# Two attention layers, a state-space block and six transformer layers in one kernel: convolution spread over more steps, other homes for its buffers, second layer's weights loaded in step 6

## The reference

```python
x = x + L0_attn(xn) + L0_ffn(xn)            # first layer, xn = layernorm(x)
xn = layernorm(x)
x = x + L1_attn(xn) + L1_ffn(xn)            # second layer

def L1_attn(x):                             # state-space block, ED = 256, K = 15, N = 16
    h = layernorm(x) * gamma + beta
    xin, z = split(h @ W_in.T + b_in)
    xc = silu(causal_conv(xin, conv_w, 15 taps, per channel) + conv_b)
    dt, B, C = split(xc @ W_x.T)
    delta = softplus(dt @ W_dt.T + b_dt)
    # scan over 2048 rows: h = h * exp(delta * A) + delta * B * xc ; y = sum(h * C)
    return x + ((y + xc * D_param) * silu(z)) @ W_out.T + b_out

def L1_ffn(x):                              # six layers
    for i in range(6):
        x = local_attention(shift_tokens(x), 16 heads of 64, window 32) + x
        x = gelu_gated_ffn(layernorm(shift_tokens(x)), inner 341) + x
    return x
```

## Time and profile before

| | us |
|---|---|
| time, median of 3 runs | 3064.14 (3058.77 to 3069.75) |
| the profiled execution's own time | 3057.84 |
| its span | 3056.0 |
| TensorE busy | 2839.6 (93%) |
| VectorE busy | 2302.5 (75%) |
| ScalarE busy | 1753.7 (57%) |
| GpSimd busy | 1673.7 (55%) |

### The profile page before, as it was taken

How to read it: one execution, slowest core, us unless ns; L and a number is a source line. 1 busy time by engine, 2 the same in 40 slices (tenths; PEclk the granted TensorE clock), 3 DMA queues, 4 the chain that set the end, 5 groups by cost and what they waited for, 6 DMA issues and landing times.

```text
span 3056.0 us, 98277 instructions
## 1 busy us (share of the span) xinstructions
PE 2839.6 (93%) x41012; PEld 1864.1 (61%) x41012; DVE 2302.5 (75%) x3659; ACT 1753.7 (57%) x2614; POOL 1673.7 (55%) x1459
## 2 busy tenths in 40 slices
PE   6999999989999998899799999999999999999996
PEld 5556556555665655566466666666666666666664
DVE  2777666584677776799577888889888888788873
ACT  2545555545666665455466666666666666666663
POOL 0000001100466665565476888788887888788862
PEclk7999999999999999999899999999999999999998
DMA  2000000000011211132324334333433343333331
GB/s 92 1 1 1 1 1 1 3 1 10 19 46 47 45 46 49 47 100 73 95 72 117 92 85 111 85 97 79 111 88 92 89 109 92 82 94 82 81 76 50
DMA packets 181801, 188.21 MB, mean 62 GB/s; under 512 B 77614, under 2 KB 128564, under 8 KB 179956
## 3 DMA queue, kind: packets, MB, share of 16 engines
q1 hardware_dynamic: 181364, 181.94, 23.5%
HBM read 60.99 MB, written 6.03 MB: 22 GB/s over the span
## 4 chain that ended last, share of the span: by engine, by line
PE 48%; issue 5%; DVE 3%; POOL 2%; ACT 1%; DMA 1%; SPq 0%; ACTq 0%; DVEq 0%; POOLq 0%
PE ps L1366 15%; PE ps L1374 5%; PE ps L1417 5%; PE ps L1459 5%; PE ps L1381 4%; PE ps L1426 2%; PE ps L1473 2%; PE ps L1480 2%; PE ps L1407 2%; PE ps L1474 2%; PE ps L1390 1%; POOL ra L2002 1%; PE ps L1443 1%; DVE ss L1854 1%; DVE acc L483 1%
## 5 line engine op out<-in xcount | busy, mean ns | idle before, releaser
L1366 PE MATMUL ps<-wqkv,xcT 128*128 128x512 f32 x1152 | 559.7, 609 | 52.5 <-issue 31.9
L594 PE MATMUL ps<-xnT,qp 128*128 128x512 f32 (+3 forms) x1280 | 529.4, 544 | 16.2 <-ACT prob L819 15.3
L1983 POOL TENSOR_TENSOR ra<-ra,rb 128x1024 f32<-128x1024 f32 x192 | 452.0, 2360 | 134.3 <-DVE rb L1847 133.6
L819 ACT ACTIVATE prob<-ps,ebias,shift 128x1024 f32<-128x1024 f32 (+7 forms) x384 | 360.4, 954 | 142.7 <-DVE ebias L710 74.3
L827 ACT ACTIVATE probT<-ps 128x512 f32<-128x512 f32 (+3 forms) x384 | 207.6, 541 | 354.4 <-PE ps L607 354.2
L594 PEld LDWEIGHTS ps<-xnT,qp 128*128 128x128 f32 x1280 | 233.0, 192 | 274.5 <-issue 228.5
L2002 POOL TENSOR_TENSOR ra<-ra,rn 128x1024 f32<-128x1024 f32 x192 | 361.3, 1902 | 7.8
L1366 PEld LDWEIGHTS ps<-wqkv,xcT 128*128 128x128 f32 x1152 | 196.2, 190 | 220.8 <-issue 209.3
L701 DVE TENSOR_REDUCE nmx<-ps 128x1 f32<-128x1024 f32 (+7 forms) x256 | 245.7, 986 | 111.1 <-PE ps L594 96.7
L1626 ACT ACTIVATE sq<-ps 128x1024 f32<-128x1024 f32 x192 | 195.1, 1016 | 93.7 <-PE ps L1366 93.4
L1845 DVE TENSOR_TENSOR ra<-ps,tab 128x1024 f32<-128x1024 f32 x192 | 233.1, 1214 | 5.9 <-issue 5.5
(11 more groups left out here) (274 smaller groups left out, 5739.0 us busy)
## 6 DMA issues: line engine op xcount, KB each, us to landing
vw<-vs SPq DMA_DIRECT2D x576, 130.0 KB
vw<-vs SPq DMA_DIRECT2D x384, 65.0 KB
bc<-bc_scratch SPq DMA_DIRECT2D x128, 128.0 KB, 3.1
area<-bc_scratch SPq DMA_DIRECT2D x128, 128.0 KB, 4.3
wqkv<-lwqkv_dram SPq DMA_DIRECT2D x6, 1536.0 KB, 8.8
xc<-xs SPq DMA_DIRECT2D x96, 32.0 KB
wo<-lwo_dram SPq DMA_DIRECT2D x6, 512.0 KB, 9.8
area<-ys SPq DMA_DIRECT2D x24, 128.0 KB
```

The costliest lines, as they stand in the source:

```text
L594: mm = E.matmul(ps[:, 2 * r + o // 512, 0:w], k.qp[:, group % 2, g % NTH * P:(g % NTH + 1) * P], k.xnT[:, k0 + o:k0 + o + w], start=True, ...
L819: A.activation(k.prob[:, r, 0:nk], ps[:, 2 * r:2 * r + 2, :].rearrange("p a b -> p (a b)")[:, 0:nk], ACT.Exp, bias=k.ebias[:, row % 2:row ...
L1366: mm = E.matmul(to[:, c, :], k.xcT[:, n % 4, :], k.wqkv[l % 2][:, at + 512 * c:at + 512 * (c + 1)], start=True, stop=True)
L1983: G.tensor_tensor(k.ra[:, n % 2, w, :], k.ra[:, n % 2, w, :], k.rb[:, w, :], ALU.add).then_inc(s("added_" + what), 1)
```

## The change

```diff
-CONV = [(0, t) for t in range(3)] + [(a, t + 3 * (1 - a)) for t in range(KC - 3) for a in (1, 0)] + ...
-CONV_FIRST, CONV_LAST = 3, 11
-IN_STEPS = {2: 0, 3: 1, 4: 2, 5: 3}
-SILU_STEP, FACTOR_STEP, RATE_STEPS = CONV_LAST + 1, CONV_LAST + 2, {CONV_LAST + 4: 0, CONV_LAST + 5: 1}
+TAPS = {3: 3, 4: 3, 5: 3, 6: 2, 7: 3, 8: 3, 9: 2, 10: 2, 11: 3, 12: 3, 13: 2, 14: 1}
+IN_EXTRA, IN_LATE = {3: 1, 4: 3}, {2: 0, 3: 2}
+HAT_STEP, SILU_STEPS, FACTOR_STEP, RATE_STEPS = 2, {9: 0, 15: 1}, 15, {16: 0, 17: 1}
...
-FIRST_UNIT = 21
+FIRST_UNIT = 22
@@ transformer_sp
-            S.wait_ge(s("conv"), ET)
+            S.wait_ge(s("saved"), 16)
         load_projections(k, l)
...
-    def save_gate(m):
-        S.wait_ge(s("in_out"), 2 * ET + 2 * m + 2)
-        S.dma_start(k.mz_d[:, m, :], k.mz1 if m else k.mz0).then_inc(s("saved"), 16)
+    def save_gates():
+        S.wait_ge(s("in_out"), 4 * ET)
+        S.dma_start(k.mz_d, k.mz).then_inc(s("saved"), 16)
...
-        if n % NT == (CONV_LAST + 1 if n < NT else 2) and n // NT + 1 < L:
+        if n % NT == (6 if n < NT else 2) and n // NT + 1 < L:
             load_layer(n // NT + 1)
...
         if n == 4:
-            save_sum()
-            save_gate(0)
-        if n == 5:
-            S.wait_ge(s("saved"), 16)
             load_forward(0)
-            save_gate(1)
-        if n == SILU_STEP:
+        if n == 5:
+            save_sum()
+            save_gates()
+        if n == max(SILU_STEPS):
             save_convolved()
-        if n == FACTOR_STEP:
+        if n == FACTOR_STEP + 1:
             save_factors()
-        if n == max(RATE_STEPS):
+        if n == max(RATE_STEPS) + 1:
             save_rates()
@@ transformer_pe
-        if n == 1:
+        if n == HAT_STEP:
             turn_hat()
-        if n in IN_STEPS:
-            E.wait_ge(s("small"), 80)
-            project_in(n, IN_STEPS[n])
+        if n in IN_EXTRA:
+            project_in("extra", n, IN_EXTRA[n])
         if n < NTILE:
             values(n, 1)
         if n + 1 < NTILE:
             turn_rows("q", n + 1)
             turn_rows("k", n + 1)
+        if n in IN_LATE:
+            E.wait_ge(s("small"), 80)
+            project_in("late", n, IN_LATE[n])
@@ transformer_act (the evictions follow their projections)
-        if n == SILU_STEP:
-            convolved()
+        if n in SILU_STEPS:
+            convolved(SILU_STEPS[n])
@@ transformer_dve, before the steps
         if n == 0:
+            V.wait_ge(s("rotated_k"), 1)
+            V.tensor_tensor(k.ra[:, 0, 1, :], k.ra[:, 0, 1, :], k.rb[:, 1, :], ALU.add).then_inc(s("added_k"), 1)
             residual_dve(k, pair("out", 0))
@@ in the steps
-        if n == 1:
-            normal_dve(k)
         if n + 2 < NTILE:
             rotate("q", n + 2)
...
-        for i in taps[2:]:
-            conv_dve(k, i)
+        for a, t in taps[2:]:
+            conv_dve(k, a, t)
+        if n == 1:
+            normal_dve(k)
@@ transformer_pool
+    G.wait_ge(s("fixed"), 32)
+    G.tensor_copy(k.band[:], k.band32).then_inc(s("band"), 1)
     for n in range(2):
         add("q", n)
         better(n)
         normal("q", n)
-        add("k", n)
+        if n:
+            add("k", n)
         normal("k", n)
-        if n == 0:
-            G.wait_ge(s("fixed"), 32)
-            G.tensor_copy(k.band[:], k.band32).then_inc(s("band"), 1)
-            G.tensor_copy(k.mxp[:, :, 0:PAD], k.tail[:]).then_inc(s("padded"), 1)
...
-        if n in (2, 3):
+        if n in (3, 4):
@@ build
-            k.mxp = here.take(P, ET, PAD + TH)
+            k.mz = here.take(P, ET, TH)
...
+            beside = here.take(P, PAD + TH)
+            k.dec = sb("dec", [P, PAD + TH], c=c)[:]
+            k.mxp = (beside, k.dec)
```

More of the change, by code:

```diff
@@ L1033 @@
 TURNED = NT // 4
-CONV = [(0, t) for t in range(3)] + [(a, t + 3 * (1 - a)) for t in range(KC - 3) for a in (1, 0)] + [(1, t) for t in range(KC - 3, KC)]
-CONV_FIRST, CONV_LAST = 3, 11
-IN_STEPS = {2: 0, 3: 1, 4: 2, 5: 3}
-SILU_STEP, FACTOR_STEP, RATE_STEPS = CONV_LAST + 1, CONV_LAST + 2, {CONV_LAST + 4: 0, CONV_LAST + 5: 1}
+TAPS = {3: 3, 4: 3, 5: 3, 6: 2, 7: 3, 8: 3, 9: 2, 10: 2, 11: 3, 12: 3, 13: 2, 14: 1}
+IN_EXTRA, IN_LATE = {3: 1, 4: 3}, {2: 0, 3: 2}
+HAT_STEP, SILU_STEPS, FACTOR_STEP, RATE_STEPS = 2, {9: 0, 15: 1}, 15, {16: 0, 17: 1}
+assert sum(TAPS.values()) == ET * KC
 def conv_share(n):
[L1042 to L1047, removed]
+    done = sum(TAPS[i] for i in TAPS if i < n)
+    return [divmod(i, KC) for i in range(done, done + TAPS.get(n, 0))]
 def heads_dve(k):
@@ L1701, in turned_hat, with projected_in, convolved @@
         A.wait_ge(s("turned"), TURNED + 3 + q)
[L1702 to L1716, removed]
+        A.activation(k.mxT[:, q * 512:(q + 1) * 512], pair("extra", HAT_STEP)[:, q, :], ACT.Identity, bias=k.cols[:, 1:2], scale=k.cols[:, 0:1]).then_inc(s("turned_out"), 1)
+    def projected_in(place, n, m):
+        for q in range(2):
+            of = pair(place, n)[:, q, :]
+            A.wait_ge(s("in_mm"), 2 * m + q + 1)
+            if m < ET:
+                A.activation(k.mxp[m][:, PAD + q * 512:PAD + (q + 1) * 512], of, ACT.Identity, bias=k.cols[:, 2 + m:3 + m]).then_inc(s("in_out"), 1)
+            else:
+                A.activation(k.mz[:, m - ET, q * 512:(q + 1) * 512], of, ACT.Silu, bias=k.cols[:, 2 + m:3 + m]).then_inc(s("in_out"), 1)
+    def convolved(a):
+        A.wait_ge(s("conv"), a + 1)
+        A.activation(k.mu[:, a, :], k.mu[:, a, :], ACT.Silu).then_inc(s("mu"), 1)
     def factors(n):
-        A.wait_ge(s("saved"), 32)
         for q in range(2):
@@ L1724, in rates @@
     def rates(n, a):
-        A.wait_ge(s("saved"), 48)
+        A.wait_ge(s("saved"), 32)
         A.wait_ge(s("dt_mm"), a + 1)
@@ L1778, in transformer_act @@
             gelu(m, int(what[2]))
[L1779 removed]
+        if n == HAT_STEP:
             turned_hat(0)
             turned_hat(1)
[L1782 to L1786 removed]
+        if n in IN_EXTRA:
+            projected_in("extra", n, IN_EXTRA[n])
+        if n in SILU_STEPS:
+            convolved(SILU_STEPS[n])
         if n + 1 < NTILE:
@@ L1791, in transformer_act @@
             out_turned(n)
+        if n in IN_LATE:
+            projected_in("late", n, IN_LATE[n])
         if n == FACTOR_STEP:
@@ L1795, in transformer_act @@
             rates(n, RATE_STEPS[n])
-        if what and what != "turn_normal" and n < NTILE or IN_STEPS.get(n, 0) >= ET:
+        if what and what != "turn_normal" and n < NTILE or IN_EXTRA.get(n, 0) >= ET or IN_LATE.get(n, 0) >= ET:
             A.preload_act_table_set("natural_log_exp_and_others")
@@ L1915, in transformer_dve @@
         taps = conv_share(n)
-        for i in taps[:2]:
-            conv_dve(k, i)
+        for a, t in taps[:2]:
+            conv_dve(k, a, t)
         if n < NTILE:
@@ L2031, in rest_sum @@
         here = k.acc[:, NTH:NT, :]
-        if step == 2:
+        if step == 3:
             G.wait_ge(s("ln_done"), 2)
@@ L2088, in transformer_pool @@
             deviations()
-        if n in (2, 3):
-            if n == 3:
+            for a in range(ET):
+                ins = G.tensor_copy(k.mxp[a][:, 0:PAD], k.tail[:, a, :])
+            ins.then_inc(s("padded"), 1)
+        if n in (3, 4):
+            if n == 4:
                 G.wait_ge(s("g"), rest)
```

40 lines of the change are left out of this document (18 added, 22 removed).

## The result

The changed kernel takes 3020.6 us (median of four runs, 3019.0 to 3029.3) where the kernel before takes 3065.3 beside it (four runs, 3058.8 to 3069.8): the ratio is 0.9862, with a 95% interval of 0.9835 to 0.9888. The profiled execution took 3019.65 us around a span of 3017.8, so the two profiles differ by 38.2 us, against 36.1 predicted. The medians of this comparison differ by 44.7, but its ratio and those of two later comparisons of the same kernels (e4, e9) are 0.9862, 0.9877 and 0.9880, which is 37 to 42 us of 3064.

The account below looks back on a forecast made before the run. The prediction took TensorE, busy 93% of the span, as the bound, with VectorE binding steps 3 to 9 and a stall in step 11. Its terms summed to -36.1 us, giving 3028 us from a median of 3064.14; range 3010 to 3047.

Parts of the forecast that it names:

- The stall: Steps 10 to 12: loading the second layer in step 6 ends GpSimd's wait for its scales and TensorE's behind it; -23.9 us.
- near 18: Sign that the prediction is right: step 11 takes near 18 us at a clock of 1.00.
- The load's price: Step 6: the second layer's load makes TensorE stand on "issue" in its value matmuls; +1.5 us, bounds 0 and 7.8.
- Norm's scaling: Steps 1 and 2: scaling behind step 1's softmax work, transposes in step 2, end the waits for GpSimd's powers; -6.4 us.
- Taps: Steps 3 to 9: convolution taps spread over steps 3 to 14 shorten steps where VectorE is late; -5.7 us, bounds 0 and -12.5.
- steps 4 to 6 each below 18.2: Sign that the prediction is right: steps 4, 5 and 6 each take less than 18.2 us.
- Steps 13 to 18: These steps gain three taps and one half's SiLU; +1.5 us (0.5 SiLU, 1.0 step 13's two taps), bounds -4 and +7.
- Band's cast: Start of the second part: the mask's cast ahead of GpSimd's first addition ends TensorE's 3.14 us stand; -3.1 us.
- the later scan: All 64 scan units one step later, with the same instructions; 0 us, bounds -5 and +5.
- (a): Rival, steps 3 to 14: long TensorE steps pay back VectorE's lateness, 10 us more, -46, 3018 us; chance 0.13.
- (b): Rival: trailing taps wait for GpSimd's additions in seven steps (3, 4, 5, 7, 8, 11, 12), 2.0 us each; 3042 us; chance 0.13.
- (c): Rival: only the stall of step 11 and its clock go, -20, VectorE stays as late; 3044 us; chance 0.08.

Follow-up runs that it names:

- e4: The changed kernel itself, run again beside the kernel before: 3024.0 us, ratio 0.9877.
- e9: The changed kernel itself, run once more beside the kernel before: 3023.1 us, ratio 0.9880.
- e3: The changed kernel with the second layer's whole load moved back from step 6 to step 12: 3036.3 us, ratio 0.9918 to the kernel before.
- e1: The kernel before with only the second layer's scales' transfer moved to step 6, weights still in step 12: 3041.6 us, ratio 0.9933.
- e6: The changed kernel with the norm's scaling back ahead of step 1's rotations, its transposes staying in step 2: 3027.8 us, ratio 0.9895 to the kernel before.
- e11: The changed kernel with the second layer's whole load in one go in step 8 instead of 6: 3020.3 us, ratio 0.9864 to the kernel before.
- e10: The changed kernel with the second layer's scales in step 6, its weights in four pieces in steps 7 to 10: 3018.8 us, ratio 0.9860.
- e12: The changed kernel with its load in pieces and one tap moved from step 5 to step 14: 3015.4 us, ratio 0.9847 to the kernel before.
- e5: The changed kernel with the old distribution of taps (4, 4, 4, then six times 3, steps 3 to 11): 3027.3 us, ratio 0.9890.
- e2: The kernel before with only the scan's first unit moved from step 21 to step 22: 3059.3 us, ratio 0.9992.
- e7: The changed kernel with the mask's cast behind the first keys' normalising and their addition on GpSimd again: 3025.0 us, ratio 0.9883 to the kernel before.

## Why the prediction was right, and where it was off

**The stall (-23.9; measured -23.5): right, mechanism and size.** Put back alone it costs 20.8 us in step 11 (e3), taken away alone it gives 20.5 there (e1). Step 11 is 18.85 us at a clock of 1.00, with "near 18" expected, and steps 10 and 12 are 19.4 and 18.4 for 19.7 and 18.3.

**The load's price (+1.5; measured 3.2 to 4.3): the mis-sized term.** It was taken from one stand of 1.5 us beside the third layer's load in step 18. The same step of the kernel before has a second one, and as much moving as step 6 has now:

```profile
1600.55:1623.40 22.85, 18.86 (x355) 13.92 (x356) 13.36 (x20) 8.70 (x13) 17.19 (x19) 1.00 0.72 206
...
PE ps L1417 <- issue: 1.5, 1, 1.5
PE ps L1381 <- issue: 1.4, 1, 1.4
```

So the row was half of what that load cost there, and 22.85 us is 2.8 more than the 20.0 that step 18 takes after. The prediction also left out the clock: the stand of 2.75 us in step 6 put the transposes behind it at half the clock, 1.2 us more.

**Norm's scaling (-6.4; measured -6.7): right in sum.** Step 1 is 17.5 for 16.4 and step 2 17.8 for 19.2: step 2 absorbed more of the transposes than was booked, and step 1 paid VectorE's 17.26 us of work, which is 1.5 more than the 15.72 it was priced by. One instruction explains it. The scaling's first half, 1.23 us where nothing ran beside it, now stands beside GpSimd's two additions and takes 3.03:

```profile
1255.12 4.70 POOL L1980 TENSOR_TENSOR ra<-ra,rb 128x1024 f32<-128x1024 f32 x2
...
1257.87 3.03 DVE L1095 TENSOR_TENSOR ys<-ys,st 128x1024 f32<-128x1024 f32 x1
```

e6 shows that the order of that one piece of work is the whole of the gain.

**Taps (-5.7; some -2 to -3).** With the load's 3.8 taken off, steps 3 to 9 are 129.7 us, 1.9 less than before; in e11 and e10, where the load costs nothing, 129.4 and 128.6. Step 6 did come to 17.0 (e3, e11). Steps 4, 5, 7 and 9 are 0.6 to 0.9 longer than booked: step 5's trailing tap was priced by the median and takes 2.50 us in the changed kernel's first profile and 2.96 in e10. Where it moved away, the step lost 2.9 (e12). Of the signs on record, "steps 4 to 6 each below 18.2" came true for step 4 alone (18.1; steps 5 and 6 take 18.8 and 21.2). The lower bound of the term, -12.5, is also more than TensorE's busy time leaves: 131.63 less 121.22 is 10.4.

**Steps 13 to 18 (+1.5; measured -4.5).** The 1.0 for step 13's two taps was booked in the wrong place. They stand ahead of step 13's max, so they lie in the row of step 12, which was priced with three taps already; the row of step 13 has one tap, and takes 16.5 us with it, 17.3 without (e5) and 17.7 with two (e12). Step 18 takes 20.0 us for 22.9. Most of that isn't the change's merit: e1 and e2, without the rest of the change, have 21.0 and 21.4 there, so the one profile of before had a long step 18. The other 1.0 to 1.3 us seem to be the change's, since ten of its eleven kernels' profiles have 20.0 to 20.1 and only e4's has 21.7; no run tells why.

**Band's cast (-3.1; measured -4.2 and -4.5, after and e7), the later scan (0; 0 by e2).** Right.

So the sum was near (-36.1 for -38.2) partly because two errors cancelled: the steps with the load and the taps gave 6 us less than booked, steps 13 to 18 gave 6 us more, of which some 1.5 to 2 are scatter of the one profile (22.9 against 21.0 and 21.4). That much of the nearness is luck.

**The rivals.** (a) Lateness paid back, 3018: the time lies nearer to it than to 3028, but it isn't what happened, since steps 3 to 9, where it had to show, gave less and not more. (b) Trailing taps beside GpSimd's additions, 2 us each in seven steps: not in seven, but in step 5 it did, with 2.50 to 2.96 us in all nine profiles of the changed kernel and its variants that keep its three taps there. The Trainium skill, "SBUF — State Buffer", section "Who interferes with whom", has a VectorE instruction with two inputs in SBUF and a GpSimd one that reads SBUF block each other; the traces agree, with 2.96 us for the tap of step 5 in e10, and 2.62 for the first keys' addition on VectorE, begun 0.36 us behind GpSimd's instruction. The scaling in step 1, at 3.03 us for 1.23, is a third. What (b) had wrong is how often the two meet. (c) was wrong by what steps 1, 2 and the start gave.

## What to carry to other kernels

Ask how many steps ahead an engine wants its smallest input, and issue it by itself: a transfer of 128 KB behind one of 2 MB that had to wait for its buffer cost 20 us, and moving it alone took that away. Then try a bulk load at more than one place, and in pieces: in one piece it cost 3.2 to 4.3 us in step 6, two steps later nothing, in pieces nothing. Look for stands on "issue" of the engine that binds, and count all of them in a step. And price an instruction of the engine that binds a step by the duration it has at that place: one that stands beside another engine's work on the same memory may cost over twice its median.

## What the runs showed of the hardware

- A stand of TensorE costs more than itself. After 2.75 us of it, 16 transposes took 3.17 us for 1.97, and the step's mean clock was 0.92; after 19.1 us (e3) it was 0.74 over the step. TensorE ran at its lower level, 1.2 GHz, behind either (0.50 from 1352.0 to 1354.5 us in the changed kernel), and at 2.4 GHz through steps 10 to 18 of the changed kernel (1.00), which have no such stand.
- A load of 2 MB beside matmuls cost TensorE 3.2 to 4.3 us in one place (step 6, 340 GB/s while it ran) and nothing in another (step 8 of e11, 334 GB/s), with no engine and no semaphore to show for it.
- Stands of TensorE on "issue" follow the 16 KB transfers of the queue "instruction": 90 of 90 stands of 0.8 us or more ended 1.2 to 1.6 us behind the end of one. Beside the load in step 6 that transfer started 2.3 to 3.1 us later than without it.
- A VectorE instruction with both inputs in SBUF beside a GpSimd instruction: 2.96 us for 1.28 (a tap), 3.03 for 1.23 (the scaling), each ending 1.1 us behind GpSimd's.
- Sixteen steps with the scan took 291.66 and 288.99 us after, 290.81 and 288.63 before: which step of the pattern a unit falls on made no difference.
